# A tile's weight fetch is issued by SyncE instead of ScalarE

## The reference

```python
x = x + xattn(layernorm(x), ctx, ctx, Wq, Wk, Wv, Wo)   # softmax within each 64-key block, summed over blocks
xf = layernorm(x).reshape(-1, D)
top1 = argmax(softmax(xf @ gate_w.T))                    # one of 2 routed experts
masked = xf[None] * one_hot(top1).T[:, :, None]
h = relu(einsum('end,edh->enh', masked, w1) + b1[:, None, :])          # hidden size 1024
routed = (einsum('enh,ehd->end', h, w2) + b2[:, None, :]).sum(axis=0)
x = x + routed + relu(xf @ sw1 + sb1) @ sw2 + sb2
```

## Time and profile before

| | |
|---|---|
| timed runs, median (lowest to highest) | 1034.85 us (1033.58 to 1035.83) |
| profiled execution | 1025.89 us |
| its span | 1024.1 us |
| TensorE matmul busy | 876.7 us |
| ScalarE busy | 450.5 us |
| GpSimd busy | 491.5 us |
| VectorE busy | 536.4 us |
| moved by DMA | 159.69 MB |

### The profile page before, as it was taken

The page is one execution under the profiler, slowest core; times in us unless marked ns, Lnnn a source line. Parts: engine busy times, 40 slices in busy tenths (PEclk is TensorE's granted clock), DMA queues, the critical chain, the costliest instruction groups (busy, mean ns, idle before and its releaser), DMA issues.

```text
span 1024.1 us, 22039 instructions
## 1 busy us (share of the span) xinstructions
PE 876.7 (86%) x7751; PEld 732.4 (72%) x7751; DVE 536.4 (52%) x1090; ACT 450.5 (44%) x991; POOL 491.5 (48%) x798
## 2 busy tenths in 40 slices
PE   3377788998989898998989898989999898978897
PEld 2154666685859687786868696877868686957897
DVE  6556456383727465573837373655638372715200
ACT  3151443444454544444444545444444445442553
POOL 6442524254454636364544546363645545452553
PEclk8576797999999999999999999999999999989999
DMA  8866572909375583919193755839191937444600
GB/s 236 194 200 159 166 177 62 262 27 283 58 254 94 182 166 102 243 55 263 42 280 62 251 98 184 165 99 249 52 264 41 279 61 262 67 168 160 250 11 11
DMA packets 90481, 159.69 MB, mean 156 GB/s; under 512 B 8448, under 2 KB 80512, under 8 KB 85840
## 3 DMA queue, kind: packets, MB, share of 16 engines
q1 hardware_dynamic: 76432, 77.92, 35.0%
q10 hardware_dynamic: 4032, 58.72, 14.6%
q0 software_dynamic: 9984, 22.61, 7.8%
HBM read 119.84 MB, written 39.38 MB: 155 GB/s over the span
## 4 chain that ended last, share of the span: by engine, by line
PE 36%; DMA 16%; issue 16%; POOL 14%; DVE 6%; ACT 2%; SPq 1%; ACTq 1%; POOLq 1%; DVEq 0%
DMA rowin<-queue 9%; PE hid L467 9%; PE acc L675 9%; POOL hl L1337 7%; PE num L540 4%; PE den L547 3%; PE work L522 3%; PE work L587 2%; DMA QP<-scratch_m 2%; DMA queue<-rows,pos 2%; POOL rstd L1329 2%; PE work L573 2%; ACT PT L841 2%; POOL x1b L1344 2%; DMA scratch_m<-mT 1%
## 5 line engine op out<-in xcount | busy, mean ns | idle before, releaser
L1337 POOL TENSOR_TENSOR hl<-h,hh 128x256 fp32r<-128x256 f32 x272 | 203.4, 764 | 223.8 <-ACT hh L862 223.7
L1026 DVE TENSOR_REDUCE nmax<-work 128x8 f32<-128x512 f32 x256 | 163.0, 682 | 25.5 <-PE work L507 25.1
L841 ACT ACTIVATE PT<-work 128x512 f32<-128x512 f32 x256 | 134.0, 604 | 90.6 <-PE work L522 90.3
L1032 DVE COPY T<-num 128x512 f32<-128x512 f32 x64 | 44.2, 691 | 221.7 <-PE num L540 221.7
L522 PE MATMUL work<-QP,KP 128*128 128x256 f32 x512 | 97.0, 312 | 56.5 <-ACT PT L841 34.8
L522 PEld LDWEIGHTS work<-QP,KP 128*128 128x128 f32 x512 | 71.9, 195 | 89.9 <-ACT PT L841 48.4
L862 ACT ACTIVATE h<-hid,bias 128x256 f32<-128x256 f32 x160 | 76.9, 481 | 115.6 <-PE hid L467 114.6
L507 PE MATMUL work<-KP,QP 96*128 96x512 f32 x256 | 99.1, 465 | 30.1 <-DMA QP<-scratch_q 18.5
L467 PE MATMUL hid<-XS,WS 128*128 128x256 f32 x768 | 109.3, 293 | 3.6 <-DVE idle L1194 3.6
L467 PEld LDWEIGHTS hid<-XS,WS 128*128 128x128 f32 x768 | 101.8, 199 | 5.8 <-DVE idle L1194 4.5
L467 PE MATMUL hid<-XR,WR 128*128 128x256 f32 x672 | 90.7, 284 | 0.8 <-issue 0.8
(11 more groups left out here) (238 smaller groups left out, 1665.5 us busy)
## 6 DMA issues: line engine op xcount, KB each, us to landing
WR<-wx ACTq DMA_DIRECT2D x28, 2048.0 KB, 11.2
KP<-scratch_k SPq DMA_DIRECT2D x96, 128.0 KB, 7.6
QP<-scratch_q SPq DMA_DIRECT2D x96, 128.0 KB, 9.1
scratch_k<-T SPq DMA_DIRECT2D x16, 512.0 KB, 3.3
scratch_q<-T SPq DMA_DIRECT2D x16, 512.0 KB, 2.9
wx<-WR POOLq DMA_DIRECT2D x16, 512.0 KB, 4.3
stages<-wraw POOLq DMA_DIRECT2D x24, 256.0 KB, 4.7
xin<-x SPq DMA_DIRECT2D x16, 256.0 KB, 10.2
```

The source lines that it names most:

```text
L841: nc.scalar.activation(PT[:, j % 8].rearrange("p t q -> p (t q)"), work[:, BANK[("st", j)], :], ACT.Exp).then_inc(sem["exp_done"], 1)
L1026: nc.vector.tensor_reduce(nmax[:, t, 8 * p:8 * p + 8], work[:, BANK[("s", j)], :].rearrange("q (b k) -> q b k", k=BLOCK), AX_X, ALU.max, n ...
L1032: nc.vector.tensor_copy(T[:, 2 * v:2 * v + 2, :], num[:, :, :]).then_inc(sem["num_copied"], 1)
L1337: nc.gpsimd.tensor_tensor(R(hl[:, k % 2, a]), h32[:, k % 2, a], hh[:, k % 2, a], ALU.subtract).then_inc(sem["hl_done"], 1)
```

## The change

`load_weights` moves from ScalarE to SyncE. There it stands behind the bounces of the next tile's keys and queries and ahead of `load_tile`; the two DMAs so go from queue q10 to q1. The wait on `proj_lo` becomes one on `ident_loaded`, both long reached; all other waits are the same. ScalarE goes from exponential 3 straight to exponential 4.

```diff
@@ block.sync
+            def load_weights(i):
+
+                selected, = held(sp, sp_counts, i - 1)
+                sp.wait_ge(sem["ident_loaded"], 16)
+                sp.wait_ge(sem["sel_done"], selected)
+                if type(i) is int and i == 2:
+                    sp.wait_ge(sem["wx_stored"], 16 * (PIECES - SHARED_PIECES))
+                expert = sp.value_load(control[0:1, 1:2], min_val=0, max_val=1)
+                if type(i) is not int or i > 2:
+                    sp.wait_ge(sem["w2_done"], unit_no(i, RU - 1) + 1)
+                for h in range(2):
+                    sp.dma_start(WR[:, 2 * h:2 * h + 2].rearrange("p k a b c -> p (k a b c)"),
+                                  wx[bass.ds(expert * P, P), 2 * h:2 * h + 2].rearrange("p k a b c -> p (k a b c)")) \
+                        .then_inc(sem[f"wr_loaded{h}"], 16)
+
             def iteration(i, more, loads=True):
                 shift(i)
                 if more:
                     bounces(i + 1)
+                if type(i) is not int or i >= 2:
+                    load_weights(i)
                 if type(i) is not int or i >= 2:
                     load_tile(i)
@@ block.scalar
-            act_counts = [act.alloc_register("act_count")]
...
-            def load_weights(i):
-
-                selected, = held(act, act_counts, i - 1)
-                act.wait_ge(sem["proj_lo"], 4)
...
                 for j in range(4):
                     exps(i, j)
-                if type(i) is not int or i >= 2:
-                    load_weights(i)
                 for v in range(VISITS):
```

## The result

The changed kernel takes 1019.71 us (median of four, 1019.2 to 1023.05) against 1034.98: a ratio of 0.9874 (95% interval 0.9854 to 0.9894), 15.3 us faster where 18 were forecast. A second measurement on another chip gave 0.9856 (0.9819 to 0.9894).

The account below looks back on a forecast made before the run. TensorE fills 86% of the span, but a tile is set by its cycle with ScalarE and by the DMA work. The smaller gain per tile sums to 18.1 us, from 1034.85 to 1017 us, range 1009 to 1036.

Parts of the forecast that it names:

- The two cycles: Steady loop: TensorE with ScalarE, and the DMA work, two cycles of nearly equal length, together set a tile's 56.3 us.
- ACT loses load_weights: ScalarE between exponentials 3 and 4: drops 1.85 us; TensorE's 1.65 us wait shrinks to about 0.1, saving up to 1.55 a tile.
- SP gains load_weights: SyncE behind the queries' bounce: weights issued 1.9 us earlier, at no cost as SyncE idles; nothing queued behind is issued later.
- The queue, 1.3 us a tile: Shared DMA queue: weights, rowin and queries all land 1.3 us earlier a tile, between bounds of 1.2 and 1.9.
- The sum: Smaller of 1.55 (TensorE) and 1.3 (transfers) a tile: 13 x 1.3 + 1.2 = 18.1 us, giving 1017 us.
- Rival A: Transposes of rowin: TensorE waits there for what it won at the exponentials; 1035 us, or 1043 unhidden; chance 0.13.
- Rival B: Append gets stuck in the weights, delaying rowin's issue; rowin lands 1.6 us later, 1046 to 1057 us; chance 0.11.
- the place behind the bounce of the queries: Weights on SyncE start behind this bounce, not at its issue; the reason for taking 1.3 us, near the lower bound.

Follow-up runs that it names:

- E6: Changed kernel, but SyncE waits for the tile's append before issuing the weights, still ahead of rowin: 1.0237 of the kernel before, 1055.15 us.
- E1: The kernel before, unchanged, timed and profiled again against itself: ratio 1.0005, span 1028.2 us.
- E10: Changed kernel, but each weight fetch brings only half its bytes, so the result is not the reference's: 0.9582 of the kernel before.
- E5: Changed kernel, but ScalarE still stops between exponentials 3 and 4, with the selection wait and three value loads: 0.9908 of the kernel before.
- E2: The changed kernel, unchanged, timed and profiled again on another chip: 0.9856 of the kernel before, 1015.47 us, span 1010.2 us.
- E7: Changed kernel, but SyncE issues the weights' second half behind the spreads and the context's fetch: 0.9591 of the kernel before, 990.97 us.
- E3: Kernel before, but ScalarE issues the weights in its own queue ahead of its first exponential, not behind the fourth: 1.0795, 1111.58 us.
- E8: Changed kernel, but SyncE issues the weights between the bounces of keys and queries: 1.1030 of the kernel before, 1138.6 us.
- E9: Kernel before, but SyncE issues the weights' second half behind the spreads and the context's fetch; ScalarE keeps the first half: 0.9680.

## Why the prediction was right, and where not

*The two cycles.* Right for the transfers: a later start costs much though ScalarE is free (E6: 1.7 us later in a tile, the loop's tile 1.9 us longer than in E1), and with the transfers out of the way the changed kernel is at 0.9582 (E10). ScalarE's part is less sure. The early start alone gives 0.9908 (E5), both give 0.9856 to 0.9874, and this difference is within the intervals; ScalarE freed with the weights at their old place was not tried. One row was misread: the 7.0 us in 7 waits of the earlier trace rows hold 3.0 us in the tail, where TensorE waits for VectorE (xhat, which reads rowin). TensorE waited for rowin itself in 6 tiles, 4.1 us. The sum does not use this number.

*ACT loses load_weights.* Right: exponential 4 starts 0.49 us behind exponential 3 in every tile, as forecast, and the stop at score 7 is gone, where 0.1 was forecast.

*SP gains load_weights.* The issue came 1.88 us behind the bounce, not 1.4; the waits and the value load took 1.50 us, which I had priced at 1.05 by load_tile's. That what stands behind on SP would not be issued later was wrong: rowin went out 4.8 us later against the bounce, for the append landed 7.6 us behind its issue where it was 2.7.

*The queue, 1.3 us a tile.* This is the term that was mis-sized. The weights came earlier by more than forecast (1.8 and 1.9 us in the means), rowin by about as much (1.2 and 1.4), but the queries only by 0.1 and 0.9. From the last weights to rowin it was 0.9 us in the mean and is 1.5. The DMA packets show a part of why: in the kernel before, rowin's 256 packets went out from 9.7 us behind the bounce on, and 211 of them started before the weights' last packet ended (means of the loop); in the changed kernel the first goes out at 14.9 us, and only 50 do. One queue alone does not explain the 0.6 us: E6 has one queue too, and rowin lands 0.9 us behind the weights there. E6 issues rowin 2 us behind the weights and not 8.6, and POOL's scatter out<-yr, in the changed kernel still moving until 16.5 us, is through before its weights end. Which of the two it is, and why the queries came so little earlier, stays open.

*The sum.* The loop of E2 won 0.86 us a tile over E1, that of the first pair none, or 0.4 without the tile of 60.1 us; 1.3 were forecast. The timed difference of 15.3 us is 1.1 for each of the 14 tiles only if all of it is laid on them. Of E1 and E2, 8.6 us of 18.0 lie outside the 11 tiles measured, where the sum has 3.8 for what is not these 11. That 15.3 came so near to 18 is in part luck.

*Rival A* took place in part: TensorE waits for rowin in all 14 tiles, where it did in 6.

*Rival B*'s mechanism is real, the late append, but not its price. rowin, issued at 354.12 in E2, needed 6.85 us, and 2.8 in E7, where the first half of the weights is through by then: it stood behind the weights for some 4 us. In E6 nothing of the weights runs beside the append, and rowin lands 0.9 us behind the weights in place of 1.5; so an estimate of what a prompt append could bring is 0.6 us a tile. No run sped up the append with the weights at the same place.

*What I did not see.* I counted the place behind the bounce of the queries as a loss. It keeps the weights off the bounce. In the changed kernel and in E2 the last packet of the bounce is through 2.6 us behind its issue in the loop, and the first packet of the weights follows at 2.8 to 3.1. In E3, issued 0.1 us behind the bounce, and in E8, issued ahead of it, the weights run beside or before it, the bounce lands some 15.6 us behind its issue, and VectorE stands still. E3 changed the place in time and the queue together, and its first two fetches, in the other queue but later, held nothing back. So the place in time explains these runs; whether one queue protects the bounce as well is not shown, for ScalarE's queue was not tried at 1.9 us. The Trainium skill (DMA: Bandwidth & Descriptors, Issuing engines are not separate DMA queues) says that DMAs from several engines interleave on the same 16 DMA engines and that another issuing engine only saves the sequencer's time. The interleaving agrees with the packets of E3; the second statement no run here tests by itself.

## What to carry to other kernels

A queue's order is a schedule. Put large transfers behind the small ones that somebody waits for soon, and cut them so that each part is issued in order of when it is needed. The move with that order took 4.1% here (E7), the move alone 1.3%, and the order alone, with ScalarE still issuing the first half, 3.2% (E9). Before freeing an engine, find the deadline of the next transfer on the path; a stop may already be hidden by it (E5: 15 us more waiting cost some 3 to 5 us). Before starting a big transfer earlier, look at what is in flight at that moment, in every queue, and who waits for it.

## What the runs showed of the hardware that was not expected

Small transfers suffered far beyond their size beside the 16 KB packets of the weights: the append went from 2.7 us (before) to 7.6 (E2), the bounce of 512 KB from 2.9 us (before) to 15.6 (E3).

TensorE's granted clock fell to 0.50 of full speed (1.2 GHz) behind some of its stops. In the kernel before, after the stop of 1.66 us before 294.15, stretches of 2 us, with clock, DMA share and GB/s as the last columns:

```profile
294.00:296.00 2.00, 1.85 (x18) 1.11 (x22) 0.00 (x0) 2.00 (x6) 1.74 (x3) 0.70 0.82 303
296.00:298.00 2.00, 2.00 (x21) 0.67 (x13) 0.69 (x1) 1.02 (x3) 1.83 (x5) 0.50 0.97 383
```

It did so in every second tile of the kernel before (clock 0.97 over the tile, 1.00 in its neighbour). The tiles were nearly equally long, 56.5 us on average with the fall and 56.1 without it; in E1 they were 56.4 and 56.5. The DMA share is near 1 in these stretches, so the transfers can have hidden it; that is argued, not shown. In the changed kernel it fell once in the loop, at the longest wait for the queries there:

```profile
542.90 1.22 PE L524 MATMUL work<-KP,QP 96*128 96x512 f32 x2 [2.72 <-DMA QP<-scratch_q]
```
```profile
544.00:546.00 2.00, 2.00 (x11) 2.00 (x10) 1.67 (x4) 0.22 (x1) 0.00 (x0) 0.50 0.01 4
```

That tile took 60.1 us where its neighbours took 56.3 and 55.8. Hardly a transfer was in flight then that could have hidden it (DMA share 0.01). How much of the tile's length is the clock's was not measured by itself. In E2 it fell once in the loop too, behind a wait of 2.23 us for rowin.
